# Carrying expert gates to the inner units: one row spread by DMA in place of four transposes per tile

## The reference

```
# block 2: 16 experts of 128 units, weights dequantised from integers
z = jnp.einsum('th,ehi->tei', x, w_up)
a = jnp.square(jnp.maximum(z, 0.0))
aw = a * wdense[:, :, None]
# block 3: 8 experts of 176 units, and a shared network of 704 units
h = silu(einsum('th,ehi->eti', x, w_gate)) * einsum('th,ehi->eti', x, w_up)
routed = einsum('eth,te->th', einsum('eti,eih->eth', h, w_down), combine)
shared_out = sigmoid(x @ shared_gate_w)[:, None] * shared
return routed + shared_out
```

## Time and profile before

| | |
|---|---|
| median of 3 runs | 5421.03 us (5420.83 to 5429.38) |
| span of the profiled execution (the page gives no time beside it) | 5423.2 us |
| TensorE busy | 5193.4 us, 96% of the span |
| VectorE, ScalarE, GpSimd busy | 3246.3, 2765.4, 1900.2 us |
| DMA | 114.60 MB, mean 21 GB/s over the span |
| f2, from its first to its last matmul | about 3864 to 4118 us of the span |
| f3, from its first to its last matmul | about 5034 to 5418 us |

### The profile page before, as it was taken

One profiled execution on the slowest core, in us unless ns is written; L12 is line 12 of the kernel. 1 busy time (PEld: TensorE's weight loads), 2 busy tenths in 40 slices (PEclk: granted clock), 3 DMA queues, 4 the chain that ended last, 5 costly groups with the idle time before them and its releaser, 6 DMA issues. The chain is left out here.

```text
span 5423.2 us, 138613 instructions
## 1 busy us (share of the span) xinstructions
PE 5193.4 (96%) x58674; PEld 3455.6 (64%) x58674; DVE 3246.3 (60%) x7451; ACT 2765.4 (51%) x6000; POOL 1900.2 (35%) x2353
## 2 busy tenths in 40 slices
PE   6999999999999989999999999999898999999999
PEld 3666666666666665777777654333466677677565
DVE  6899999999999953444444338664444444444222
ACT  5888888888878832555555312666412222222111
POOL 4888888888888830000000002000000111111000
PEclk8999999999999989999999998999999999999999
DMA  1000000000000000000000000000101211221100
GB/s 32 7 8 12 7 8 7 8 7 7 12 7 25 3 2 12 13 11 15 13 11 11 26 0 8 1 1 1 63 1 42 69 62 69 69 68 62 54 4 8
DMA packets 34216, 114.60 MB, mean 21 GB/s; under 512 B 4416, under 2 KB 9792, under 8 KB 33600
## 3 DMA queue, kind: packets, MB, share of 16 engines
q1 hardware_dynamic: 33600, 105.74, 5.7%
HBM read 103.63 MB, written 2.10 MB: 19 GB/s over the span
## 5 line engine op out<-in xcount | busy, mean ns | idle before, releaser
L719 POOL TENSOR_TENSOR d_kq<-d_kq,d_tot 128x512 f32<-128x512 f32 x448 | 526.8, 1176 | 93.0 <-PE d_lpd L323 65.1
L825 DVE SCALAR_TENSOR_TENSOR d_qkv<-d_fr,d_wts,d_qkv 128x509 f32<-128x509 f32 (+2 forms) x576 | 427.3, 742 | 35.0 <-ACT d_qkv L663 16.0
L2019 DVE TENSOR_REDUCE r_nm<-r_ps 128x2 f32<-128x1024 f32 x256 | 307.6, 1222 | 141.8 <-PE r_ps L1838 141.7
L1240 POOL TENSOR_TENSOR f1rstd<-f1var,mhalf 128x4 f32<-128x4 f32 x4 | 4.0, 1010 | 1091.0 <-DVE f1var L1265 1091.0
L312 PE MATMUL d_fr<-xnT,d_wts 128*128 128x512 f32 x768 | 371.8, 608 | 11.2 <-DVE d_qkv L825 5.9
L2117 PE MATMUL e_pj<-xnT,e_wts 128*128 128x512 f32 x768 | 348.1, 603 | 11.7 <-DMA e_wts<-in_w3all 10.4
L1939 ACT ACTIVATE r_pT<-r_ps 128x512 f32<-128x512 f32 x512 | 274.9, 598 | 149.8 <-PE r_ps L1846 149.3
L723 POOL TENSOR_TENSOR d_kF<-d_kF,d_tot 128x256 f32<-128x256 f32 x448 | 305.8, 683 | 116.1 <-PE d_lpd L323 111.2
L1470 PEld LDWEIGHTS c_po<-c_pT,c_vt 128*128 128x128 f32 x2304 | 294.7, 191 | 21.0 <-ACT c_pT L1535 9.2
L1573 DVE TENSOR_TENSOR c_sc<-c_sc,c_mask 128x128 f32<-128x128 f32 x256 | 76.7, 300 | 383.2 <-PE c_sc L1425 383.2
L1470 PE MATMUL c_po<-c_pT,c_vt 128*128 128x128 f32 x2304 | 301.9, 276 | 0.2
(11 more groups left out here) (501 smaller groups left out, 13365.5 us busy)
## 6 DMA issues: line engine op xcount, KB each, us to landing
e_wts<-in_w3all SPq DMA_DIRECT2D x64, 897.0 KB, 4.5
d_wts<-in_headw SPq DMA_DIRECT2D x16, 583.5 KB, 3.8
c_wqo<-in_wqo SPq DMA_DIRECT2D x32, 256.0 KB, 2.6
f3ws<-in_f3w SPq DMA_DIRECT2D x17, 384.0 KB, 7.3
f2ws<-in_f2s SPq DMA_DIRECT2D x16, 256.0 KB, 6.2
f2qs<-in_f2q SPq DMA_DIRECT2D x16, 256.0 KB, 7.0
f1ws<-in_f1w SPq DMA_DIRECT2D x8, 384.0 KB, 6.4
f0w<-in_f0w SPq DMA_DIRECT2D x6, 384.0 KB, 5.8
```

The lines of the kernel that those rows point to most:

```text
L719: return nc.gpsimd.tensor_tensor(v, v, bc(bc(by_pair(u, lv)[:, :, 0], 2, h), 1, 2), ALU.mult)
L825: return nc.vector.scalar_tensor_tensor(into, fr[:, x // 2, 0:GRP - 3 + i], tap(u, x, i), into, ALU.mult, ALU.add)
L2019: nc.vector.tensor_reduce(nm[:, t % 2, half, 4 * j + i0:4 * j + i0 + 2], ps[:, row_pair(row - 1):row_pair(row - 1) + 2], AX, ALU.max).then ...
```

## The change

The tile `side`, `blocks`, ScalarE's `widen` and the four transposes per step are taken out. In their place, ahead of step 0, TensorE transposes each 128-token block of the gates once (16 transposes in a stage), and ScalarE copies the result to a tile `gate_rows`: one gate row of 2048 tokens per partition, 16 rows in f2 and 9 in f3 (the ninth is the shared network's gate, which now stands in `T.w3`). For each step SyncE issues a DMA that reads the 512 tokens of one row, 2 KB on one partition, 128 times over, and writes them to all 128 partitions of `wide`, one of four buffers. In f3 seven of a group's 17 tiles straddle two experts; these take two DMAs, of 16 to 112 partitions each. The DMA of step `n` waits for `hid` of step `n - 4`. VectorE's first product now waits for the DMA and reads `wide` from SBUF instead of `side` from PSUM.

```diff
+        WIDE = 4
+        gT = gate_rows = wide = None
+        if gates is not None:
+            NR = gates.shape[2]
+            gT, gate_rows, wide = psum("gT", [P, 2, GRP]), sb("gate_rows", [P, B * S]), sb("wide", [P, WIDE, GRP])
...
+                def widen(n):
+                    g, t = divmod(n, NTL)
+                    sp.wait_ge(rows_ready, g + 1)
+                    for row, p0, p1 in rows_of(t):
+                        sp.dma_start(wide[p0:p1, n % WIDE, :], bc(gate_rows[row:row + 1, g * GRP:(g + 1) * GRP], 1, p1 - p0)).then_inc(wide_loaded[n % WIDE], 16)
...
                 for t in range(0 if ternary else NTL):
                     sp.dma_start(ws[:, t], w[t]).then_inc(loaded[t], 16)
                     if raw is not None:
                         sp.dma_start(qs[:, t], raw[0][t]).then_inc(loaded[t], 16)
+                    if gates is not None and t < WIDE:
+                        widen(t)
...
+                if gates is not None:
+                    for n in range(WIDE, TOTAL):
+                        sp.wait_ge(hid_ready, n - WIDE + 1)
+                        widen(n)
+                        if out is not None and n % NTL == 2 + WIDE and n >= NTL:
+                            store(n // NTL - 1)
...
+                if gates is not None:
+                    for g in range(NG):
+                        if g >= 2:
+                            pe.wait_ge(rows_ready, g - 1)
+                        for j in range(NC):
+                            last = nc.tensor.transpose(gT[0:NR, g % 2, j * P:(j + 1) * P], gates[:, g * NC + j, :], T.ident[:])
+                        last.then_inc(gates_turned, 1)
...
-                    if side is not None:
-                        if blocks is not None:
-                            pe.wait_ge(widened, n + 1)
-                        for k in range(NC):
-                            column = weigh(g * NC + k, t) if weigh else wide[:, n % 3, k]
-                            last = nc.tensor.transpose(side[:, n % 2, k * P:(k + 1) * P], column, T.ident[:])
-                        last.then_inc(wide_mm, 1)
...
+                if gates is not None:
+                    for g in range(NG):
+                        act.wait_ge(gates_turned, g + 1)
+                        nc.scalar.activation(gate_rows[0:NR, g * GRP:(g + 1) * GRP], gT[0:NR, g % 2], ACT.Copy).then_inc(rows_ready, 1)
...
-                        dve.wait_ge(wide_mm, n + 1)
-                        ch.link(nc.vector.tensor_tensor(h, act1[:, n % 2], side[:, n % 2, :], ALU.mult))
+                        dve.wait_ge(wide_loaded[n % WIDE], wide_at[n])
+                        ch.link(nc.vector.tensor_tensor(h, act1[:, n % 2], wide[:, n % WIDE, :], ALU.mult))
```

More of the change, by code:

```diff
@@ L1093, in _, with feed_forward @@
                 ch.link(nc.vector.reciprocal(T.ternary[:], T.ternary[:]))
-BLK = 16
-EX, SH = 8 * 176 // BLK, 704 // BLK
-def feed_forward(nc, T, name, NTL, kind, w, weigh=None, blocks=None, prepare=None, raw=None, ternary=False, out=None, norms=NG):
+def feed_forward(nc, T, name, NTL, kind, w, gates=None, rows_of=None, prepare=None, raw=None, ternary=False, out=None, norms=NG):
     parts = 1 if kind == "relu2" else 2
@@ L1116, in feed_forward @@
         pg, py = psum("pg", [P, 2, parts, GRP]), psum("py", [P, 2, GRP])
-        side = psum("side", [P, 2, GRP]) if weigh or blocks is not None else None
         flip = psum("flip", [P, 2, GRP]) if out is None else None
-        wide = sb("wide", [P, 3, NC, P]) if blocks is not None else None
-        loaded = [sem(f"loaded{t}") for t in range(NTL)]
[L1121 to L1125, removed]
+        WIDE = 4
[3 more added lines that the diff above has]
+            gT, gate_rows, wide = psum("gT", [P, 2, GRP]), sb("gate_rows", [P, B * S]), sb("wide", [P, WIDE, GRP])
+            wide_loaded = [sem(f"wide_loaded{i}") for i in range(WIDE)]
+            gates_turned, rows_ready = sem("gates_turned"), sem("rows_ready")
+            landed, wide_at = [0] * WIDE, []
+            for n in range(TOTAL):
+                landed[n % WIDE] += 16 * len(rows_of(n % NTL))
+                wide_at.append(landed[n % WIDE])
+        loaded = [sem(f"loaded{t}") for t in range(NTL)]
+        g_loaded, prepared, stored = sem("g_loaded"), sem("prepared"), sem("stored")
+        up_mm, act_ready, hid_ready, y_part, added = sem("up_mm"), sem("act_ready"), sem("hid_ready"), sem("y_part"), sem("added")
         dve_steps, centred, squared, var_ready, rstd_ready = sem("dve_steps"), sem("centred"), sem("squared"), sem("var_ready"), sem("rstd_ready")
@@ L1137, in _, with store @@
                         sp.dma_start(qs[:, t], raw[0][t]).then_inc(loaded[t], 16)
+                    if gates is not None and t < WIDE:
+                        widen(t)
+                def store(g):
+                    sp.wait_ge(added, g + 1)
+                    sp.dma_start(out.rearrange("(t p) d -> p t d", p=P)[:, g * NC:(g + 1) * NC], T.x[:, g * NC:(g + 1) * NC]).then_inc(stored, 16)
+                if gates is not None:
[4 more added lines that the diff above has]
+                            store(n // NTL - 1)
                 if out is not None:
-                    for g in range(NG):
-                        sp.wait_ge(added, g + 1)
-                        sp.dma_start(out.rearrange("(t p) d -> p t d", p=P)[:, g * NC:(g + 1) * NC], T.x[:, g * NC:(g + 1) * NC]).then_inc(stored, 16)
+                    store(NG - 1)
                     sp.wait_ge(stored, 16 * NG)
@@ L1224, in _ @@
                     nc.scalar.activation(act1[:, n % 2], pg[:, n % 2, 0, :], func).then_inc(act_ready, 1)
-                    if blocks is not None and n + 2 < TOTAL:
-                        widen(n + 2)
                     if out is None and g and t == 2:
@@ L1269, in normalise @@
                     nc.vector.tensor_tensor(xn[:], xn[:], bc(rstd[:], 2, D), ALU.mult).then_inc(xn_ready, 1)
[L1271 to L1274, removed]
                 if raw is not None:
@@ L1291, in _ @@
                     h = hid[:, n % 3]
-                    if side is None:
+                    if gates is None:
                         nc.vector.tensor_tensor(h, act1[:, n % 2], pg[:, n % 2, 1, :], ALU.mult).then_inc(hid_ready, 1)
                     else:
-                        dve.wait_ge(wide_mm, n + 1)
-                        ch.link(nc.vector.tensor_tensor(h, act1[:, n % 2], side[:, n % 2, :], ALU.mult))
+                        dve.wait_ge(wide_loaded[n % WIDE], wide_at[n])
+                        ch.link(nc.vector.tensor_tensor(h, act1[:, n % 2], wide[:, n % WIDE, :], ALU.mult))
                         nc.vector.tensor_tensor(h, h, act1[:, n % 2] if kind == "relu2" else pg[:, n % 2, 1, :], ALU.mult).then_inc(hid_ready, 1)
@@ L1630, in two_best @@
         ch.link(nc.vector.reciprocal(tot[:], tot[:]))
-        TTS(weights[:], p[:], bc(tot[:], 2, E), ALU.mult)
+        TTS(weights, p[:], bc(tot[:], 2, E), ALU.mult)
 H2, G2, D2 = 16, 2, 16
@@ L2036, in _ @@
                             dve.wait_ge(late_loaded, 64)
-                            two_best(nc, ch, E2, p, e1, key, sel, both, top, tot, order, T.w2, 1e-20)
+                            two_best(nc, ch, E2, p, e1, key, sel, both, top, tot, order, T.w2[:], 1e-20)
                 for t in range(12, 16):
@@ L2326, in _ @@
                     if ROUTE + 3 <= n < ROUTE + 7:
-                        two_best(nc, ch, E3, p, e1, key, sel, both, top, tot, order, T.w3, 0, parts=(n - ROUTE - 3,))
+                        two_best(nc, ch, E3, p, e1, key, sel, both, top, tot, order, T.w3[:, :, 0:E3], 0, parts=(n - ROUTE - 3,))
                     if n == ROUTE + 7:
                         dve.wait_ge(shared_ready, 1)
-                        for copy in range(2):
-                            ch.did(nc.vector.tensor_scalar(T.shared[:, :, copy], zs[:], 0.5, 0.5, ALU.mult, ALU.add))
+                        nc.vector.tensor_scalar(T.w3[:, :, E3], zs[:], 0.5, 0.5, ALU.mult, ALU.add)
 def build_program(nc, ins, out, stages):
@@ L2341, in build_program @@
         T.ternary = sb("ternary", [P, 3])
-        T.w2, T.w3, T.shared = sb("w2", [P, NT, E2]), sb("w3", [P, NT, E3]), sb("shared", [P, NT, 2])
+        T.w2, T.w3 = sb("w2", [P, NT, E2]), sb("w3", [P, NT, E3 + 1])
         T.out = out
@@ L2380, in dequantise, with rows_of @@
         return nc.vector.tensor_scalar(w[:, D:], w[:, D:], gs[:, 1:2], None, ALU.mult)
-    feed_forward(nc, T, "f2", E2, "relu2", ins["f2s"], weigh=lambda c, e: T.w2[:, c, e:e + 1].to_broadcast([P, P]),
+    feed_forward(nc, T, "f2", E2, "relu2", ins["f2s"], gates=T.w2, rows_of=lambda e: [(e, 0, P)],
                  prepare=dequantise, raw=(ins["f2q"], ins["gs"]))
 def ffn3(nc, T, ins):
-    with nc.sbuf_tensor("f3_blocks", [P, NT, 17 * P // BLK], F32) as blocks:
-        feed_forward(nc, T, "f3", 17, "silu", ins["f3w"], blocks=blocks, out=T.out)
+    def rows_of(t):
+        row = lambda unit: min(unit // 176, E3)
```

(3 more changed lines are left out.)

## The result

The changed kernel took 5976.75 us (median of 4 runs, 5971.31 to 5981.93) against 5423.92 for the kernel before (5420.83 to 5429.38): ratio 1.1021, 95% interval 1.1006 to 1.1036, so 553 us slower. The forecast was 6170 us, slower by 746, with a range from 5360 to 6410.

What follows compares the result with a forecast made beforehand. TensorE, busy 96% of the span, was taken to bound the kernel. With gate DMAs of 10.18 us per step setting the pace, f2's +420 us and f3's +326 on 5421 gave 6170 us, range 5360 to 6410.

Steps and rivals of the forecast that it cites:

- The bound: TensorE bounds f2 and f3; without transposes its steps are 3.44 and 5.16 us, 58.1 us less in all.
- The deciding term: Gate DMAs in f2 and f3: reading 262,144 bytes from one partition takes 10.2 us per step and sets the pace.
- The chosen sixteenth: Path out of one partition passes one engine's share of 412 GB/s, 25.8 GB/s; chance 0.50.
- The sum: Steps of 10.18 us plus loads and stage ends: f2 +420 us, f3 +326, together +746, giving 6170 us.
- between: Rival, chance 0.08: a partition passes 28 to 60 GB/s or, second ground, DMAs of neighbouring rows overlap; 5500 us.
- the period is about 10.2 us in both stages: Sign of being right: f2 and f3 share this period although f3 has half again as much TensorE work.
- the last sign: If the DMA's time differs between f2 and f3, the limit follows which rows are in flight, not each transfer.
- likeliest case: Gate DMAs in f2 and f3 at a sixteenth per partition: 6170 us, by itself 6070 to 6410, chance 0.50.
- The clock: TensorE's granted clock falls below 1.00 in f2 and f3, costing about nothing or up to 10 us.
- The stall at step 4: In f2, gate DMA 4 issued behind 32 loads lands late: under 5 us once.
- Full rate: Rival, chance 0.25: engines read the row side by side, TensorE stays the bound in f2 and f3; 5369 us.
- Slower yet: Rival, chance 0.17 for above 6410 us: one partition passes half an engine's share, 12.9 GB/s, 20.4 us per step; 7510 us.

Runs made afterwards that it cites:

- run 1: Changed kernel, but each of the 128 partitions of the buffer is filled from the same partition of another tile, gates not applied: 5375 us.
- run 6: Changed kernel, but the copied rows are first stored to HBM and each step's DMA reads its row there: 5376 us.
- run 9: run 6 with gate DMAs issued among the weight loads, the first four behind loads 3 to 6: 5363 us.
- run 5: Changed kernel with 1 KB in place of 2 KB read per partition written, so gates not the right ones: 5429 us.
- run 2: Changed kernel with copies of each gate row; even steps read partition r, odd steps r + 32: 5985 us.
- run 3: Changed kernel with copies of each gate row; even steps read partition r, odd steps r + 64: 5551 us.
- run 7: Changed kernel with copied rows; each step uses four DMAs of 32 partitions, from r, r + 16, r + 64 and r + 80: 5388 us.

## Why the prediction was right, and where its sum was off

*The bound, right.* Transposes gone, TensorE's step is 3.44 and 5.16 us, as worked out from the earlier trace rows: runs 1, 6 and 9 show these periods to 0.01 us. The 58 us are real where the DMA is hidden (run 9 gains 57.6).

*The deciding term, right in kind.* The path out of one partition sets the pace, VectorE waits for `wide`, and the wait reaches TensorE. Run 1 shows that it is the reading side and run 5 that it is bytes. The chosen sixteenth (25.8 GB/s, from the earlier trace rows) was measured at 262,144 B / 9.65 us = 27.2 GB/s, and the Trainium skill's estimate ("SBUF — State Buffer", section "Door 1: The DMA port swizzle (why [64,N] ≈ [32,N])", 9.6 us) was the closer one. That section also puts partitions 32 apart on one port and 64 apart on two, and runs 2 and 3 agree. That the sixteenth came so close is partly luck: it was one engine's share of the best load rate, picked between two far ends, and runs 2 and 3 show a path that belongs to a group of partitions.

*The sum, 193 us too high.* From the first load to the last matmul f2 took 561.8 us against 679 forecast, and f3 639.3 against 714. The price per step was too high by 132 x (10.18 - 9.65) = 70 us. The other 123 us (86 in f2, 37 in f3) are steps shorter than 9.65 us, a term that the forecast had left out and named only under its rival "between": neighbouring transfers do overlap where their rows lie on different paths. In f2 every fourth step is short; in f3 rows change less often. So the sign "the period is about 10.2 us in both stages" failed (8.42 and 9.26 us in the mean), and the last sign, that a difference between f2 and f3 follows from which rows are in flight, pointed to the cause.

The loads and the ends of the stages came out as forecast in their total: 21.6 + 16 us and twice 6 make 50 us, and 50 were measured. The steps behind the loads lost 8.5 us (f2, 18.13 us) and 10.6 us (f3, 20.28) above 9.65. In f2 the loads also held up the start: the first product stands 25.9 us after the first load, on VectorE behind a dequantisation that waits for its own load.

```profile
3879.19 0.69 DVE L2383 SCALAR_TENSOR_TENSOR f2ws<-f2qs,f2ws 128x512 f32<-128x512 int32 x1 [8.11 <-DMA f2qs<-in_f2q]
3880.45 0.68 DVE L1302 TENSOR_TENSOR f2hid<-f2act,f2wide 128x512 f32<-128x512 f32 x1
```

*The range.* 5977 us lies in the stated range, but that range spans three cases. It is below the likeliest case's own 6070 to 6410 us and above the rival "between" (5500): the time of this case was missed for want of the overlap, and the width of the range covered it.

*The clock, right.* It fell to 0.81 and 0.87 in the windows above and cost little, since the DMAs were later still: about 2 us at the end of each stage, where the last second layer took 3.79 us in place of 1.7 (f3).

```profile
5963.70 3.79 PE f3py L1171 x8
```

*The start, under-priced.* The stall at step 4 was put under 5 us and lies in the rival's margin; run 1 measured 8.1 us, in f2 alone. SyncE's blocked issues (7 to 9 us) were not foreseen.

*The rivals.* "Full rate" fell with the first trace, and run 1 shows what it would have looked like. "Slower yet" fell with 27.2 GB/s. The experiments' own rivals, a price per transfer or per read, fell with runs 1 to 3 and 5. "Between" was right in its second ground, the overlap of neighbouring rows, and wrong in its rate.

## What to carry to other kernels

A DMA that spreads one SBUF row over 128 partitions is priced by the bytes that leave one place, not by the engines' total: here 27 GB/s, 9.65 us for 256 KB, while the same bytes read from 128 partitions were hidden behind steps of 3.44 us. Ask of each transfer how many places it reads, and if it is one, let it read from HBM, or from copies on partitions 64 apart (16 apart together with 64 as in run 7), several within one step. And place what the pipeline needs first ahead of the bulk loads in the issuing queue: between runs 6 and 9 the gain over the kernel before grew from 48.6 to 57.6 us that way.

## What the runs showed of the hardware that was not expected

- Whole transfers that alternated between four groups of partitions were hardly faster than between two (4.82 and 4.91 us per step in f2, each about half of 9.65), though pieces of 32 partitions from the same four kept up with steps of 3.44 us (run 7).
- DMA share is no measure of bytes: 0.88 at 32 GB/s in the changed kernel, 1.03 to 1.05 at 388 to 412 GB/s in the earlier trace rows.
- An issue on SyncE's queue is not always short: a gate DMA behind others took up to 11.9 us to issue in f2 and 13.4 in f3 (medians 7.3 and 6.0), and so what stands behind it is late before it reaches any engine.
- In steady state 128 reads of one 2 KB row of HBM land in 3.4 us, against 2.3 us for as many bytes from 128 partitions (run 1).
